# Four cross-attention layers on one core: the rest of a pair's keys in one tile, its transposes in 64 columns, and both phases in one block

## The chip, the cores and the metric

The kernel runs on one core of a Trainium2 chip. The metric is the device time of one execution in microseconds (us), the median of the runs.

## The reference

A stream x of 8 batches x 512 tokens x 512 channels goes through four cross-attention layers, each of which attends to the same context of 8 x 77 tokens of width 1024 and adds its result to the stream.

```python
# layers 0 and 2 (16 heads of 64, below "wide")
q, k, v = x @ Wq, ctx @ Wk, ctx @ Wv
logits = einsum(q, k) * 64 ** -0.5
logits[:, token_indices_A] += -20 * (1 - mask_A)      # the same for B
x = softmax(logits) @ v @ Wo + bo + x
# layers 1 and 3 (16 query heads of 32, 4 key/value heads, below "narrow")
q, k, v = rmsnorm(x) @ wq, ctx @ wk, ctx @ wv
x = softmax(q @ k.T * 32 ** -0.5) @ v @ wo + x
```

All is fp32. The kernel reaches that accuracy on TensorE by splitting each operand into a high part (fp32r, a copy by ScalarE) and a low part (the difference, by VectorE or GpSimd) and by adding three products: high x high, high x low, low x high (`three_passes`, L228).

## The kernel before

**The first block** (`context_block`, L254) computes keys and values of the context, for both wide layers in eight pairs of weight blocks and for both narrow ones in a ninth (`NJ` = 9 rounds j). A round is 96 key matmuls of 308 columns and 120 value matmuls of 256 columns. ScalarE and VectorE drain each bank into a high and a low part, and SP stores them to the scratch tensors `k_scr`, `v_scr`, `k1_scr`, `v1_scr` (L340 to L353). SP also loads the weights one round ahead (L329). In the last round it loads x of batch 0 into one half of the weight buffer (L331), then two blocks of query weights (L333, L335), of which the second waits until x has been split (`late_lo`, L334). ScalarE's queue in the last round is: drain the keys, split those two weight blocks (`split_late`, L386), drain the five value banks (L383); VectorE's has the same order, and TensorE's last group of value matmuls waits for VectorE's first drain (L519). SP waits at the end for all stores (L355, L356). The block ends on all engines.

**The second block** (`attention_block`, L545) runs the four layers. Its work is cut into units: one batch and one group of four heads, so 4 units a batch, 32 a layer, 128 in all (`NU`). Units of layers 0 and 2 are of kind A (wide, two chunks of 128 channels), those of 1 and 3 of kind B (narrow, one chunk). Each engine goes through steps s = 0 ... 129 in an order written out by hand (`STEPS`). In step s TensorE does:

- the scores of unit s, in 4 tiles of 128 tokens (`scores`), alternating over two banks. For a wide unit ScalarE writes the bias of the masked tokens into the bank first (`bias`, L939), and tile t + 2 can get its bias only when VectorE has subtracted the maximum of tile t out of the same bank (L944, L1059);
- the queries of unit s + 1 (`queries`), 24 or 12 matmuls of 512 columns, beside the first two tiles;
- the value matmuls of unit s - 2 (`values`, L790), beside the other two;
- three groups of four transposes of unit s - 1 (`turn`, L778), each group into one bank;
- the output projections of a batch (`project`, L810). For a wide batch all four, 96 matmuls, stand in one step out of four (`projections`, L145).

A unit has 4 x 77 = 308 probability columns per token, which don't fill 128-row blocks. Transposes n = 0 and 1 turn 128 columns each. What is left (26 columns of each pair of heads of a wide unit, 52 of a narrow one) goes through transpose n = 2 (`TWICE`): GpSimd copies these columns twice, side by side, into the tile `rest` (L1205, L1210), so that the transposed bank has them in its rows 0 to 63 and again in 64 to 127. ScalarE copies the whole bank as the high part (L974), VectorE replaces rows 64 to 127 by the difference (L1074). One value matmul with the high values in both halves then gives high x high and low x high, a second with the low values gives high x low. So a wide unit has 2 chunks x (3 + 2) = 10 value matmuls, a narrow one 3 + 3 + 2 = 8. The values come in from `v_scr` in small DMAs on SP (`load_vals`, L653; the list `pieces` from `value_pieces`, L64), 8 for a wide unit.

ScalarE's order in a wide step (L1014 to L1031) is: query copy 0, bias 2, query copy 1, bias 3, exponentials of tiles 0 and 1, output copy 0, transposed bank 0, bias 0 of the next step, output copy 1, bank 1, bias 1 of the next step, bank 2, exponentials of tiles 2 and 3, new x. VectorE's (L1121 to L1141) is: maximum and subtraction of tile 0, query 0, tile 1, query 1, tile 2, output 0, rest of bank 0, tile 3, rest of bank 1, output 1, rest of bank 2, sums and reciprocals, results of the projections. GpSimd multiplies the probabilities by the reciprocals (`normalise`, L1193), makes the two copies, and computes low parts of x and of weights.

Of the kernel before, what the change touches and what calls it, by code (L numbers as in the profile page):

```python
# [13 lines left out]

# [5 lines left out]
F32 = mybir.dt.float32  # L20
# [6 lines left out]
P = 128  # L27
# [30 lines left out]

TWICE = 2
# [4 lines left out]
def value_pieces(outs):  # L64

    blocks, pieces = [], []
    if outs == 2:
        for m in range(2):
            first, rest = len(blocks), len(blocks) + 1
            blocks += [(m, m), (TWICE, m)]  # L70
            row = REST_A * m + P - (PAIR - REST_A)
            pieces += [(2 * m, 0, CTX, first, 0, 2), (2 * m + 1, 0, P - CTX, first, CTX, 2),
                       (2 * m + 1, P - CTX, CTX, rest, row, 2), (2 * m + 1, P - CTX, CTX, rest, 64 + row, 1)]
        return blocks, pieces
    blocks = [(0, 0), (1, 0), (TWICE, 0)]
    for n in range(2):
        for h in range(GH):
            lo, hi = max(h * CTX, n * P), min((h + 1) * CTX, n * P + P)
            if lo < hi:
                pieces.append((h, lo - h * CTX, hi - h * CTX, n, lo - n * P, 2))  # L80
    row, t0 = 2 * P - (SC - REST_B), 2 * P - (GH - 1) * CTX
    pieces += [(GH - 1, t0, CTX, TWICE, row, 2), (GH - 1, t0, CTX, TWICE, 64 + row, 1)]
    return blocks, pieces
# [37 lines left out]
class Plan:  # L121
# [23 lines left out]
    def projections(self, s):  # L145
# [12 lines left out]
        return found  # L158

# [94 lines left out]
def context_block(nc, lasting, ctxT, kvw, k_scr, v_scr, k1_scr, v1_scr, x_in, wqA, boA, normB, masks, tokens,  # L254
# [5 lines left out]
    with ExitStack() as ctx:  # L260
# [6 lines left out]
        ctx_raw = sb("ctx_raw", [P, KC, ROWS], F32)  # L267
        ctx_s = sb("ctx_s", [P, 2, KC, ROWS], F32R)
        w_raw = sb("kvw_raw", [P, 2, PART], F32)
        k_out = sb("k_out", [P, 2, 2, ROWS], F32R)  # L270
        v_out = sb("v_out", [P, len(VROWS), 2, BLK], F32R)
        banks = [ctx.enter_context(nc.psum_tensor(f"ctx_bank{i}", [P, 512], F32)) for i in range(8)]

        w_A, x_s, ident, mean_w, mhalf = lasting.w_s, lasting.x_s, lasting.ident, lasting.mean_w, lasting.mhalf
        bias_s, bo, nw = lasting.bias_s, lasting.bo, lasting.nw
        w_s = w_A[:, 2:4]
        tok_i = sb("tok_i", [P, 8], I32)
        tok_f = sb("tok_f", [P, 2, 8], F32)

        mask_b = sb("mask_b", [P, 2, TILES], F32)  # L280
        iota_t = ctx_raw[:, 2, 0:CTX]
        cmp_t = [ctx_raw[:, 2, CTX * (1 + n):CTX * (2 + n)] for n in range(3)]

        ctx_loaded = [sem(f"ctx_loaded{n}") for n in range(KC // 2)]
        first_loaded = [sem(f"first_loaded{n}") for n in range(KC // 2)]
        first_hi, first_lo = sem("first_hi"), sem("first_lo")
        w_loaded = [sem("kw_loaded"), sem("vw_loaded")]
        ctx_hi, ctx_lo = sem("ctx_hi"), sem("ctx_lo")
        w_hi, w_lo = [sem("kw_hi"), sem("vw_hi")], [sem("kw_lo"), sem("vw_lo")]
        k_mm, v_mm = sem("k_mm"), sem("v_mm")  # L290
        k_hi, k_lo, v_hi, v_lo = sem("k_hi"), sem("k_lo"), sem("v_hi"), sem("v_lo")
        k_stored, v_stored = sem("k_stored"), sem("v_stored")
        consts, cleared, setup_loaded, chain = map(sem, ("consts", "setup_cleared", "setup_loaded", "dve_chain"))
        late_loaded = [sem("x_first"), sem("wq_first"), sem("wq_second")]
        late_hi, late_lo = sem("late_hi"), sem("late_lo")
        NV = len(VROWS)
        FULL = sum(r == P for r in VROWS)

        def late_parts(n):
            if n == 0:  # L300
                return [x_s[:, 0, h].rearrange("p k n -> p (k n)") for h in range(2)]
            return [w_A[:, n - 1, h] for h in range(2)]

        def keys_stored(j):
            return 64 * j

        def vals_stored(j):
            return 32 * j

        block = ctx.enter_context(nc.Block())  # L310

        @block.sync
        def _(sp):
            for k in range(0, KC, 2):
                sp.dma_start(w_raw[:, 0, BLK * k:BLK * (k + 2)], kvw[0][:, BLK * k:BLK * (k + 2)]).then_inc(first_loaded[k // 2], 16)
                sp.dma_start(ctx_raw[:, k:k + 2], ctxT[:, k:k + 2]).then_inc(ctx_loaded[k // 2], 16)
            sp.dma_start(w_raw[:, 1], kvw[1]).then_inc(w_loaded[1], 16)
            sp.dma_start(mask_b[:, :, :], masks).then_inc(setup_loaded, 16)
            sp.dma_start(tok_i[:, :], tokens[:, ::token_words].partition_broadcast(P)).then_inc(setup_loaded, 16)
            sp.dma_start(bo[:, :, :], boA).then_inc(setup_loaded, 16)  # L320
            sp.dma_start(nw[:, :, :], normB).then_inc(setup_loaded, 16)
            for j in range(NJ):
                for slot in range(2):
                    if j == 0 and slot == 0:
                        sp.wait_ge(first_lo, KC // 2)
                    else:
                        sp.wait_ge(w_lo[slot], j + slot)
                    if j + 1 < NJ:
                        sp.dma_start(w_raw[:, slot], kvw[2 * j + 2 + slot]).then_inc(w_loaded[slot], 16)  # L329
                    elif slot == 0:  # L330
                        sp.dma_start(w_raw[:, 0], x_in[0].rearrange("p k n -> p (k n)")).then_inc(late_loaded[0], 16)  # L331
                    else:
                        sp.dma_start(w_raw[:, 1], wqA[0, 0]).then_inc(late_loaded[1], 16)  # L333
                        sp.wait_ge(late_lo, 1)  # L334
                        sp.dma_start(w_raw[:, 0], wqA[0, 1]).then_inc(late_loaded[2], 16)  # L335
                for m in range(2):
                    sp.wait_ge(k_lo, 4 * j + 2 * m + 2)
                    for h in range(2):
                        into = k_scr[j, :, :, m, h] if j < B else k1_scr[m, :, :, h]
                        sp.dma_start(into.rearrange("b q n -> q b n"),  # L340
                                     k_out[:, m, h].bitcast(F32).rearrange("q (b n) -> q b n", b=B))\
                          .then_inc(k_stored, 16)
                sp.wait_ge(v_lo, NV * j + NV)
                if j < B:
                    sp.dma_start(v_scr[j, 0:FULL * P].rearrange("(r p) s n -> p r s n", p=P),
# [981 lines left out]
```

## Time and profile before

| | us |
|---|---|
| Runs (3) | 2134.89, 2130.80, 2132.19 |
| Median | 2132.19 |
| The profiled execution's time | 2131.65 |
| Its span in the profile | 2129.7 |
| TensorE busy | 2080.0, 98% |
| VectorE busy | 1361.5, 64% |
| ScalarE busy | 927.0, 44% |
| GpSimd busy | 690.4, 32% |
| Mean granted TensorE clock | 0.995 |

The span runs from the first to the last instruction. PE is TensorE's matmuls, PEld its weight loads, DVE VectorE, ACT ScalarE, POOL GpSimd, SPq the queue of the engine that issues DMAs. Matmuls are pipelined and their ends are modelled, so start times tell more than durations. An arrow names what an instruction waited for.

### The profile page before, as it was taken

To read this page: it belongs to the slowest core of one execution; us is meant where nothing else is said; L and a number is where in the kernel's file an instruction comes from. 1 tells how busy PE (TensorE), PEld (TensorE's weight loads), DVE (VectorE), ACT (ScalarE), POOL (GpSimd) and SP (SyncE) were. 2 spreads that over 40 slices of the span, in tenths; PEclk is the share of its full clock that TensorE was granted. 3 is DMA by queue.
4 is the path that set the end of the run, shared out by engine and by line. 5 is a ranking of instruction groups with operands and counts; after the bars stand their busy time and mean duration, and the time that the engine had idled before them with its cause. 6 is when DMAs were issued, how large, how long until landed. Compare 5 with 4: busy or idle time off the path is not lost.

```text
span 2129.7 us, 31554 instructions
## 1 busy us (share of the span) xinstructions
PE 2080.0 (98%) x11674; PEld 1795.4 (84%) x11674; DVE 1361.5 (64%) x2344; ACT 927.0 (44%) x1750; POOL 690.4 (32%) x646
## 2 busy tenths in 40 slices
PE   8999999999999998999999999999999989999998
PEld 8999978888888887788888888888888877888886
DVE  5333355765576556688888675557655765888885
ACT  3222243543354334555555453335433543555552
POOL 0000043312231245465454431223122434554441
PEclk9999999999999999999999999999999999999999
DMA  7777842222222222343333332212221222233322
GB/s 213 173 158 157 179 120 74 67 62 74 54 65 63 77 60 72 85 110 100 86 95 92 102 90 67 73 55 65 63 76 51 70 72 80 67 94 88 87 71 81
DMA packets 260729, 191.02 MB, mean 90 GB/s; under 512 B 195842, under 2 KB 198306, under 8 KB 258018
## 3 DMA queue, kind: packets, MB, share of 16 engines
q1 hardware_dynamic: 260578, 189.02, 34.0%
q8 instruction: 93, 1.52, 0.3%
q14 instruction: 58, 0.48, 0.1%
HBM read 132.66 MB, written 56.26 MB: 89 GB/s over the span
## 4 chain that ended last, share of the span: by engine, by line
PE 38%; issue 31%; POOL 12%; DVE 4%; ACT 1%; SPq 1%; DMA 0%; POOLq 0%; ACTq 0%; DVEq 0%
POOL prob L1197 6%; PE acc_bank L804 6%; PE acc_bank L230 4%; PE acc_bank L232 4%; PE acc_bank L231 4%; PE t_bank L787 4%; PE q_bank L769 3%; PE q_bank L773 3%; PE q_bank L771 3%; POOL x_s L1172 3%; POOL rest L1205 2%; PE s_bank L230 2%; PE s_bank L232 2%; PE s_bank L231 1%; DVE pT_s L1077 1%
## 5 line engine op out<-in xcount | busy, mean ns | idle before, releaser
L1197 POOL TENSOR_TENSOR prob<-prob,rinv 128x1232 f32<-128x1232 f32 x128 | 288.3, 2252 | 1034.9 <-DVE rinv L1092 1034.9
L804 PE MATMUL acc_bank<-pT_s,vals_s 128*128 128x512 f32 x1152 | 369.7, 417 | 0.0
L1055 DVE TENSOR_REDUCE mx<-s_bank 128x4 f32<-128x308 f32 x512 | 243.4, 475 | 187.9 <-PE s_bank L735 117.5
L969 ACT ACTIVATE q_s<-q_bank 128x512 fp32r<-128x512 f32 x192 | 114.8, 598 | 528.7 <-PE q_bank L773 523.6
L769 PE MATMUL q_bank<-x_s,w_s 128*128 128x512 f32 x768 | 320.5, 417 | 4.0 <-POOL w_s L1190 4.0
L773 PE MATMUL q_bank<-x_s,w_s 128*128 128x512 f32 x768 | 314.6, 410 | 0.0
L771 PE MATMUL q_bank<-x_s,w_s 128*128 128x512 f32 x768 | 314.1, 409 | 0.0
L230 PE MATMUL acc_bank<-o_s,w_s 128*128 128x512 f32 x752 | 304.4, 405 | 3.0 <-DVE o_s L1083 3.0
L232 PE MATMUL acc_bank<-o_s,w_s 128*128 128x512 f32 x752 | 298.0, 396 | 0.0
L231 PE MATMUL acc_bank<-o_s,w_s 128*128 128x512 f32 x752 | 297.6, 396 | 0.0
L960 ACT ACTIVATE prob<-prob,rstd 128x308 f32<-128x308 f32 x256 | 140.0, 552 | 288.4 <-DVE prob L1059 260.6
L1059 DVE TENSOR_TENSOR prob<-s_bank,mx 128x308 f32<-128x308 f32 x512 | 244.9, 478 | 26.8 <-DVE mx L1055 0.5
L804 PEld LDWEIGHTS acc_bank<-pT_s,vals_s 128*128 128x128 f32 x1152 | 214.5, 189 | 39.5
L1077 DVE TENSOR_TENSOR pT_s<-t_bank,pT_s 128x512 fp32r<-128x512 f32 x256 | 175.6, 686 | 89.1 <-ACT pT_s L974 89.1
L974 ACT ACTIVATE pT_s<-t_bank 128x512 fp32r<-128x512 f32 x384 | 222.1, 594 | 23.8 <-PE t_bank L787 23.8
L1106 DVE SCALAR_TENSOR_TENSOR x_back<-acc_bank,bo,x_back 128x512 f32<-128x512 f32 x64 | 48.0, 750 | 248.7 <-PE acc_bank L232 248.6
L1089 DVE TENSOR_REDUCE sums<-prob 128x16 f32<-128x1232 f32 x128 | 183.2, 1431 | 3.6 <-ACT prob L952 1.6
L230 PEld LDWEIGHTS acc_bank<-o_s,w_s 128*128 128x128 f32 x752 | 141.6, 188 | 35.7 <-DVE o_s L1083 4.8
L232 PEld LDWEIGHTS acc_bank<-o_s,w_s 128*128 128x128 f32 x752 | 141.6, 188 | 34.3
L231 PEld LDWEIGHTS acc_bank<-o_s,w_s 128*128 128x128 f32 x752 | 142.0, 189 | 31.2
L773 PEld LDWEIGHTS q_bank<-x_s,w_s 128*128 128x128 f32 x768 | 146.1, 190 | 22.8
L769 PEld LDWEIGHTS q_bank<-x_s,w_s 128*128 128x128 f32 x768 | 146.6, 191 | 19.6 <-POOL w_s L1190 4.3
(105 smaller groups left out, 4086.0 us busy)
## 6 DMA issues: line engine op xcount, KB each, us to landing
stream<-x_back SPq DMA_DIRECT2D x128, 256.0 KB, 2.6
x_front<-stream SPq DMA_DIRECT2D x96, 256.0 KB, 3.3
x_back<-stream SPq DMA_DIRECT2D x96, 256.0 KB, 3.9
kvw_raw<-kvw SPq DMA_DIRECT2D x17, 1024.0 KB, 8.6
k_scr<-k_out SPq DMA_DIRECT2D x36, 308.0 KB, 8.4
keys_s<-k_scr SPq DMA_DIRECT2D x128, 77.0 KB, 2.5
v_scr<-v_out SPq DMA_DIRECT2D x8, 1024.0 KB
x_back<-x_in SPq DMA_DIRECT2D x32, 256.0 KB, 4.1
```

The costliest lines, as they stand in the source:

```text
L230: pe.matmul(out, weights[0], moving[0], start=start, stop=False)
L231: pe.matmul(out, weights[0], moving[1], start=False, stop=False)
L232: return pe.matmul(out, weights[1], moving[0], start=False, stop=stop)
L769: pe.matmul(out, w[0], x_now[0], start=k == 0, stop=False)
L771: pe.matmul(out, w[0], x_now[1], start=False, stop=False)
L773: mm = pe.matmul(out, w[1], x_now[0], start=False, stop=k == XC - 1)
L804: mm = pe.matmul(out, w, pT_s[:, part], start=i == mine[0] and part == 2 * n and w is v[0], stop=i == mine[-1] and w is terms[-1][0] and p ...
L974: act.activation(pT_s[:, 2 * n], t_bank[(3 * u + n) % 2][:, :], ACT.Copy).then_inc(t_hi, 1)
L1055: dve.tensor_reduce(top, scored, AX_X, ALU.max).then_inc(s_max, 1)
L1059: dve.tensor_tensor(prob[:, slot, t].rearrange("q (h n) -> q h n", h=GH), scored, top.unsqueeze(2).broadcast_to([P, GH, CTX]), ALU.subtrac ...
L1077: dve.tensor_tensor(pT_s[:, 2 * n + 1], t_bank[(3 * u + n) % 2][:, :], pT_s[:, 2 * n].bitcast(F32), ALU.subtract).then_inc(t_lo, 1)
L1197: pool.tensor_tensor(view, view, rinv[:, slot].unsqueeze(2).broadcast_to([P, TILES * GH, CTX]), ALU.mult).then_inc(p_norm, 1)
```

## The change

1. **Values of a wide unit.** The tile `rest` is now 64 columns wide: 32 of each pair of heads, once. The transposed bank has them in rows 0 to 31 (pair 0) and 32 to 63 (pair 1). Each pair gets a tile of its own in `pT_s` (which grows from 5 to 6 tiles): the high part in rows 0 to 31, again in 32 to 63, the low part in 64 to 95, zeros in the last 32. The values beside it are high, low, high. One value matmul per chunk does all three products: 2 x (3 + 1) = 8. ScalarE makes four copies of 32 rows where it made one, VectorE two subtractions of 32 rows where it made one, and SP issues 10 value loads where it issued 8.
2. **Transpose n = 2 in 64 columns**, for wide units from `rest`, for narrow ones straight from `prob`. GpSimd makes one copy for a wide unit, none for a narrow one. ScalarE copies 64 rows of a narrow unit.
3. **ScalarE's order** in a wide step: the exponentials of tiles 2 and 3 stand ahead of bank 2.
4. **One block.** The context's code is cut into one function per engine, called at the head of each engine's program. The attention's tiles lie over the context's, in an order that pairs a tile with one that is dead early. SP issues the first loads of attention (`begin`) in the last but one round, ahead of that round's stores. TensorE goes on to attention when all key banks are drained and the three late splits done; other engines wait for the stores only before they write over `k_out` and `v_out`.

```diff
-            row = REST_A * m + P - (PAIR - REST_A)
-            pieces += [(2 * m, 0, CTX, first, 0, 2), (2 * m + 1, 0, P - CTX, first, CTX, 2),
-                       (2 * m + 1, P - CTX, CTX, rest, row, 2), (2 * m + 1, P - CTX, CTX, rest, 64 + row, 1)]
+            row = P - (PAIR - REST_A)
+            pieces += [(2 * m, 0, CTX, first, 0, (0, 2)), (2 * m + 1, 0, P - CTX, first, CTX, (0, 2))]
+            pieces += [(2 * m + 1, P - CTX, CTX, rest, REST_A * slot + row, parts)
+                       for slot, parts in enumerate(((0, 1), (1, 2), (0, 1)))]
...
+    def sync(sp, begin):
...
+            if j == NJ - 2:
+                begin()
             for m in range(2):
                 sp.wait_ge(k_lo, 4 * j + 2 * m + 2)
...
-        pT_s = sb("pT_s", [P, 5, TOK], F32R)
-        rest = sb("rest", [P, TILES, P], F32)
+        rest = sb("rest", [P, TILES, 2 * REST_A], F32)
+        pT_s = sb("pT_s", [P, 6, TOK], F32R)
...
+            def begin():
+                sp.wait_ge(context.k_stored, context.wide_keys)
+                sp.wait_ge(context.v_stored, context.wide_vals)
+                sp.wait_ge(keys_zeroed, 2)
+                load_keys(0)
+                load_keys(1)
+                sp.wait_ge(vals_zeroed, 2)
+                load_vals(0)
+                load_vals(1)
+                load_weights(0)
+                load_weights(1)
+                for k in range(RING):
+                    load_front(1, k)
+                for m in range(XC):
+                    load_back(0, m)
+
+            context.sync(sp, begin)
             for s in range(STEPS):
+                if s == 0:
+                    sp.wait_ge(context.k_stored, context.all_keys)
+                    sp.wait_ge(context.v_stored, context.all_vals)
...
 # TensorE, turn
-                    mm = pe.transpose(t_bank[(3 * u + n) % 2][:, t * P:t * P + P], p, ident[:, :])
+                    if n < TWICE:
+                        rows, p = P, prob[:, u % 2, t, base:base + P]
+                    else:
+                        rows, p = 64, rest[:, t] if a else prob[:, u % 2, t, SC - REST_B:SC]
+                    mm = pe.transpose(t_bank[(3 * u + n) % 2][0:rows, t * P:t * P + P], p, ident[:, :])
 # TensorE, values
+                        if n == TWICE:
+                            terms = [(v[0], 2 * n + m)] if kind(u).name == "A" else [(v[0], 2 * n), (v[1], 2 * n)]
 # TensorE, start of attention
+            context.tensor(pe)
+            pe.wait_ge(context.k_lo, context.all_drained)
+            pe.wait_ge(context.late_lo, 3)
 # TensorE, a wide step
-                    beside(scores(s, 2), v, 5)
+                    beside(scores(s, 2), v, 4)
                     turned(0)
-                    beside(scores(s, 3), v, 5)
+                    beside(scores(s, 3), v, 4)
 # ScalarE, split_t
+                if n == TWICE and kind(u).name == "A":
+                    for m in range(2):
+                        for copy in range(2):
+                            e = act.activation(pT_s[REST_A * copy:REST_A * (copy + 1), 2 * n + m],
+                                               t_bank[(3 * u + n) % 2][REST_A * m:REST_A * (m + 1), :], ACT.Copy)
+                    e.then_inc(t_hi, 1)
+                    return
 # ScalarE, a wide step
                     bias(s + 1, 1)
+                    exps(s, 1)
                     turned(2)
-                    exps(s, 1)
 # VectorE, rest_t
+                if n == TWICE and kind(u).name == "A":
+                    for m in range(2):
+                        here = slice(REST_A * m, REST_A * (m + 1))
+                        e = dve.tensor_tensor(pT_s[64:64 + REST_A, 2 * n + m], t_bank[(3 * u + n) % 2][here, :],
+                                              pT_s[here, 2 * n + m].bitcast(F32), ALU.subtract)
+                    e.then_inc(t_lo, 1)
 # GpSimd, normalise
-                    for copy in range(2):
-                        ins = pool.tensor_copy(twice[:, :, copy], ends)
+                    pool.tensor_copy(rest[:, :, :].rearrange("q t (w n) -> q t w n", w=2), ends)\
+                        .then_inc(p_gathered, 1)
```

## Rows read from the trace of the kernel before

**Rows 1.** The page, part 1: busy time, share of the span, instructions.
```profile
PE 2080.0 (98%) x11674; PEld 1795.4 (84%) x11674; DVE 1361.5 (64%) x2344; ACT 927.0 (44%) x1750; POOL 690.4 (32%) x646
```

**Rows 2.** Timeline, TensorE, a wide step: start us, duration us, engine, line, operation, operands, count.
```profile
411.72 0.23 PE L729 MATMUL s_bank<-keys_s,q_s 128*128 128x154 f32 x1
411.79 0.28 PE L732 MATMUL s_bank<-keys_s,q_s 128*128 128x154 f32 x1
411.90 0.43 PE L804 MATMUL acc_bank<-pT_s,vals_s 128*128 128x512 f32 x1
...
412.24 0.44 PE L804 MATMUL acc_bank<-pT_s,vals_s 128*128 128x512 f32 x1
...
415.82 0.60 PE L787 MATMUL t_bank<-ident,prob 128*128 128x128 f32 x4
416.25 0.60 PE L787 MATMUL t_bank<-ident,rest 128*128 128x128 f32 x4
```

**Rows 3.** Timeline, ScalarE, the same step: third bank, exponentials, bias of tile 2.
```profile
405.48 0.60 ACT L974 ACTIVATE pT_s<-t_bank 128x512 fp32r<-128x512 f32 x1
405.95 0.73 ACT L952 ACTIVATE prob<-prob 128x616 f32<-128x616 f32 x1
...
410.17 0.43 ACT L945 ACTIVATE s_bank<-bias_s 128x308 f32<-128x308 f32 x1 [1.10 <-DVE prob L1059]
```

**Rows 4.** Timeline, VectorE, the same step.
```profile
405.27 0.69 DVE L1077 TENSOR_TENSOR pT_s<-t_bank,pT_s 128x512 fp32r<-128x512 f32 x1 [0.40 <-ACT pT_s L974]
405.88 0.68 DVE L1083 TENSOR_TENSOR o_s<-acc_bank,o_s 128x512 fp32r<-128x512 f32 x1
406.59 0.69 DVE L1074 TENSOR_TENSOR pT_s<-t_bank,pT_s 64x512 fp32r<-64x512 f32 x1
...
409.66 0.48 DVE L1059 TENSOR_TENSOR prob<-s_bank,mx 128x308 f32<-128x308 f32 x1
```

**Rows 5.** Timeline, a narrow step: statistics matmuls, and two bank copies in a row.
```profile
962.27 0.95 PE L850 MATMUL q_bank<-mean_w,x_power 128*128 128x1 f32 x8
...
973.94 1.08 ACT L974 ACTIVATE pT_s<-t_bank 128x512 fp32r<-128x512 f32 x2
```

**Rows 6.** Groups by line and shape, ScalarE: count, busy us, mean ns, idle before.
```profile
L383 ACT ACTIVATE v_out<-ctx_bank 128x256 fp32r<-128x256 f32 x36 | 13.6, 384 | 65.8 <-PE ctx_bank L232 65.8
...
L383 ACT ACTIVATE v_out<-ctx_bank 104x256 fp32r<-104x256 f32 x9 | 3.5, 387 | 22.9 <-PE ctx_bank L232 22.9
```

**Rows 7.** Timeline, all engines, last two context rounds and the start of attention.
```profile
208.30 3.08 SPq L329 DMA_DIRECT2D kvw_raw<-kvw  x2
...
236.49 0.43 SPq L331 DMA_DIRECT2D kvw_raw<-x_in  x1
...
244.38 1.92 ACT L389 ACTIVATE x_s<-kvw_raw 128x2048 fp32r<-128x2048 f32 x1 [7.88 <-DMA kvw_raw<-x_in]
...
269.62 0.85 PE L864 MATMUL s_bank<-x_s 128*128 128x308 f32 x2 [7.49 <-PEq L260]
...
275.92 12.50 SPq L663 DMA_DIRECT2D vals_s<-v_scr  x16
...
277.31 0.24 PE L729 MATMUL s_bank<-keys_s,q_s 128*128 128x154 f32 x1
```

**Rows 8.** Windows: length, busy us of PE, PEld, DVE, ACT, POOL; clock, DMA share, GB/s.
```profile
220.00:228.00 8.00, 8.00 (x70) 8.00 (x69) 3.53 (x4) 3.00 (x4) 0.00 (x0) 1.00 1.00 98
228.00:236.00 8.00, 8.00 (x68) 8.00 (x67) 1.27 (x3) 2.47 (x4) 0.00 (x0) 1.00 0.02 3
```

**Rows 9.** Waits of TensorE: us in total, times, longest.
```profile
PE ctx_bank L230 <- DVE v_out L429: 0.6, 1, 0.6
```

**Rows 10.** Timeline and windows, TensorE, the way into the second narrow layer.
```profile
1726.14 0.49 PE L769 MATMUL q_bank<-x_s,w_s 128*128 128x512 f32 x1 [1.98 <-POOL w_s L1190]
...
1728.00:1730.00 2.00, 2.00 (x8) 1.71 (x7) 1.20 (x3) 0.00 (x0) 1.68 (x1) 0.50 0.81 258
...
1732.99 0.34 PE L729 MATMUL s_bank<-keys_s,q_s 128*128 128x154 f32 x1 [1.01 <-ACT s_bank L945]
```

More of the change, by code:

```diff
@@ L15 @@
+from collections import namedtuple
 from contextlib import ExitStack
@@ L259, in context_block, with sb, sem @@
     assert NJ == B + 1
+    early = ExitStack()
+    def sb(name, shape, dt):
+        return early.enter_context(nc.sbuf_tensor(name, shape, dt))
+    def sem(name):
+        return ctx.enter_context(nc.semaphore(name))
+    ctx_raw = sb("ctx_raw", [P, KC, ROWS], F32)
+    ctx_s = sb("ctx_s", [P, 2, KC, ROWS], F32R)
+    w_raw = sb("kvw_raw", [P, 2, PART], F32)
+    k_out = sb("k_out", [P, 2, 2, ROWS], F32R)
+    v_out = sb("v_out", [P, len(VROWS), 2, BLK], F32R)
+    banks = [early.enter_context(nc.psum_tensor(f"ctx_bank{i}", [P, 512], F32)) for i in range(8)]
@@ new lines, in context_part @@
+    w_A, x_s, ident, mean_w, mhalf = lasting.w_s, lasting.x_s, lasting.ident, lasting.mean_w, lasting.mhalf
+    bias_s, bo, nw = lasting.bias_s, lasting.bo, lasting.nw
+    w_s = w_A[:, 2:4]
+    tok_i = sb("tok_i", [P, 8], I32)
+    tok_f = sb("tok_f", [P, 2, 8], F32)
+    mask_b = sb("mask_b", [P, 2, TILES], F32)
+    iota_t = ctx_raw[:, 2, 0:CTX]
+    cmp_t = [ctx_raw[:, 2, CTX * (1 + n):CTX * (2 + n)] for n in range(3)]
+    ctx_loaded = [sem(f"ctx_loaded{n}") for n in range(KC // 2)]
+    first_loaded = [sem(f"first_loaded{n}") for n in range(KC // 2)]
@@ new lines, in tensor, with keys, values @@
+    def tensor(pe):
+        def keys(n, k):
+            m, h = n // 2, n % 2
+            mm = three_passes(pe, banks[n][:, 0:HALF],
+                              [w_s[:, 0, s, BLK * k + m * P:BLK * k + m * P + P] for s in range(2)],
+                              [ctx_s[:, s, k, h * HALF:(h + 1) * HALF] for s in range(2)],
+                              k == 0, k == KC - 1)
+            if k == KC - 1:
+                mm.then_inc(k_mm, 1)
+        def values(r, j):
+            if NV * j + r >= 4:
+                pe.wait_ge(v_lo, NV * j + (1 if r == 4 else 0))
+            for k in range(KC):
+                mm = three_passes(pe, banks[4 + r % 4][0:VROWS[r], 0:BLK],
+                                  [ctx_s[:, s, k, r * P:r * P + VROWS[r]] for s in range(2)],
+                                  [w_s[:, 1, s, BLK * k:BLK * (k + 1)] for s in range(2)],
+                                  k == 0, k == KC - 1)
+            mm.then_inc(v_mm, 1)
+        for k in range(KC):
+            if k % 2 == 0:
+                pe.wait_ge(first_lo, k // 2 + 1)
+            pe.wait_ge(ctx_lo, k + 1)
+            for n in range(4):
+                keys(n, k)
+        for j in range(NJ):
+            if j:
+                pe.wait_ge(w_lo[0], j)
+                pe.wait_ge(k_lo, 4 * j)
+                for n in range(4):
+                    for k in range(KC):
+                        keys(n, k)
+            pe.wait_ge(w_lo[1], j + 1)
+            for r in range(NV):
+                values(r, j)
@@ L275, in context_block @@
[L275 to L308, printed above, removed]
@@ L1215, in root @@
                 pool.tensor_tensor(rstd[:, gb % 2], ms[:, gb % 2], mhalf[:, :], ALU.pow).then_inc(rstd_ready, 1)
+            context.gpsimd(pool)
+            pool.wait_ge(context.chain, context.chain_end)
             for slot in range(2):
```

532 lines of the change are left out of this document (250 added, 282 removed).

## The prediction, made before the changed kernel was run

> **What bounds the kernel now.** The page's first part comes first: TensorE is busy 98% of the span, VectorE 64% [rows 1]. Modelled matmul ends make that share unsafe, so the second view is the order in time inside one step of a wide (16-head) layer. There TensorE runs without a pause: from one value matmul to the next, with one score matmul between, 0.34 us (411.90 to 412.24); a score matmul alone 0.11 (411.79 to 411.90); so a value matmul is worth 0.23. Four transposes take 0.43 us (415.82 to 416.25), 0.108 each [rows 2]. In these steps work taken off TensorE is time, provided that the other queues keep up. How far they are behind is the third view, ScalarE's and VectorE's instructions of the same step [rows 3, 4]. TensorE needs the third score tile's bias to be in its bank; ScalarE wrote it from 410.17 to 410.60, and TensorE's matmul that needs it starts at 411.72 [rows 2, 3]. So there are only 1.12 us of slack, and the bias waits for VectorE (its tile-0 subtraction ends at 410.14) [rows 4].
>
> **Part 1, TensorE in wide layers.** A wide unit has 8 value matmuls instead of 10. There are 64 wide units: 128 x 0.23 = 29.4 us less TensorE work.
>
> **Part 2, transposes with 64 columns.** The third group of four transposes of each of the 128 units turns 64 columns, not 128. Which side of a transpose costs the 0.108? The statistics matmuls move one column against 128 loaded weight columns, and eight of them still span 0.95 us, about 0.11 each [rows 5]. So at this width the weight load sets the pace. What 64 loaded columns cost no row shows. Bounds: 0.108 (nothing gained, if the moving side of a transpose is as slow) and half of that, 0.054. I take 0.06, since one-column matmuls show no moving cost: 4 x 0.048 = 0.19, say 0.18 us a unit, 11.5 us over 64 wide and 11.5 over 64 narrow units. Of the narrow ones some ten, at the start of each narrow layer and at the end, wait for VectorE anyway: 54 x 0.18 = 9.7 us.
> The Trainium skill (TensorE: Matmul & The Clock Gate, "LDWEIGHTS") says that a weight load takes its columns divided by 1.2 GHz, whatever the rows; for 128 columns that is 107 ns, and the trace agrees with 108 [rows 2]. By it 64 columns would take an estimated 53 ns, and this part would come to 14 and 12 us instead of 11.5 and 9.7.
>
> **Part 3, the split of the rest in wide units.** This runs against the change. Before, ScalarE makes one copy of the third transposed bank and VectorE one subtraction. Now ScalarE makes four copies, each of 32 partitions x 512, and VectorE two subtractions of 32 x 512; the last half of the exponentials goes ahead of the copies, and VectorE's sums still stand behind its subtractions. Do fewer partitions cost less? No: ScalarE's 104x256 copy took 387 ns and its 128x256 copy 384 [rows 6]; VectorE's subtraction over 64 partitions (406.59) and over 128 (405.27) both took 0.69 [rows 4]. Back to back two ScalarE copies take 1.08, so each further one adds 0.49 [rows 5].
> Walk the chain in the step of rows 3 and 4. At 405.48 ScalarE now starts the exponentials, 0.73 long less the 0.12 by which its instructions overlap (0.60 long, 0.49 apart), so 0.61, then four copies: 405.48 + 0.61 + 3 x 0.49 + 0.60 = 408.16. VectorE, which took up the rest at 406.59, takes it up at 408.18: 1.59 late. The second subtraction adds 0.61 (405.27 to 405.88): 2.20 late. Sums, reciprocals and the next tile 0 follow in its queue, so the bias of tile 2 is done at 410.60 + 2.20 = 412.80. TensorE reached the step's end earlier: the chain starts 0.46 earlier (two value matmuls; 412.34), TensorE's wish for scores 2 comes 0.64 earlier (also the transposes; 411.08). A stall of 412.34 - 411.08 = 1.26 us per step, where there was none. What is queued behind the waiting score matmul on TensorE: the value matmuls, the transposes of the unit before, and through them ScalarE and VectorE; nobody catches up by it, because VectorE's other tiles follow TensorE.
> The stall appears where VectorE comes late into a step. In wide layers the projections of a batch stand in one step of every four (96 matmuls x 0.23 = 22 us), behind which VectorE is idle again; the step after it has no stall. Three in four steps stall, and the first ones of a wide layer not: 2 x 23 x 1.26 = 58.0 us. Together with parts 1 and 2: wide layers 58.0 - 29.4 - 11.5 = +17.1 us. Units 30 and 31 of each wide layer carry the long split into narrow steps: +1.
> Bounds for the four copies: if each took only the 0.36 of the 308-column work (a bias of 0.43 less the usual overlap), the stall is 0.74 and the wide layers -7; if copies of one bank don't overlap (0.60 each), 1.7 and +37.
> GpSimd: one copy less in wide units, two less in narrow ones, 0.37 each. Its normalisation starts 2.2 later, ends before TensorE's transposes need it (they are later by the stall as well). Cost nothing. Two more value loads per wide unit on SP, 0.78 us each (16 in 12.50 [rows 7]): ten take 7.8, the keys 1.2, in a step of over 11, and values are loaded a whole step ahead; nothing.
>
> **Part 4, one block.** Now TensorE idles 7.49 us between the blocks, from 262.13 to 269.62, and the first score of attention is at 277.31 [rows 7]. Without the gap, and with the two openers (0.3) and 24 query matmuls at 0.23 (5.5): 267.8, 9.5 us less; the slow restart is in that. But the loads that attention needs are now issued by SP at the last but one key/value pair, behind the weight load that it issues up to 211.4: 20 value DMAs (15.6 us at 0.78), 4 for keys and 9 of 256 KB (some 2.5 and 4.2), so until about 233.7 [rows 7]. SP stores the keys of that pair only then. Before, these stores were through by 228, at 98 GB/s; then the DMA engines were idle until 236 [rows 8]. Now four stores of 308 KB start at 233.7 behind the last 256 KB loads: 1.23 MB at 98 to 150 GB/s is 8 to 12 us, so the value store and the load of x_in, issued at 236.49 and landed at 244.38 before [rows 7], come 8 to 11 us late. Behind x_in hang its split, then the last weight load, its split, and only then VectorE's drain of the last values, and TensorE already waits for that drain now (0.6 us) [rows 9]. So TensorE idles some 9 us before its last 24 context matmuls, and restarts at the lower clock as it does now (+2): -9.5 + 9 + 2 = +1.5. Bounds: -9.5 (the stores hide in the idle stretch) and +6 (13 us late).
> The Trainium skill (DMA: Bandwidth & Descriptors, "Queues, rings and completion order") says that a ring is consumed in order and a completion counts only after every earlier write. If x_in passed the stores, part 4 would be -9.5; by the rule it can't.
>
> **The sum.** 17.1 + 1 - 9.7 + 1.5 = +9.9 us on the profiled execution's 2131.65 (its span is 2129.7), so 2141.6. That execution is 0.54 under the median of 2132.19: 2142.
>
> **Rivals.**
> A. The stall never comes and TensorE stays the bound: -29.4 - 11.5 - 9.7 + 1.5 = -49.1, 2083 us; faster. For it: today's waits in wide steps are nearly nil. Against: the slack is 1.12 us and the added queue work 2.20. It decides at a delay under 0.9 us. Chance 0.22.
> B. The forecast. Own range 2133 to 2158. Chance 0.42.
> C. The stores hide, part 4 brings its 9.5: 2131, no change. Against: SP's queue order. Chance 0.12.
> D. The transposes cost what they did: the stall is 1.08, 46 x 1.08 - 29.4 + 1 + 1.5 = +22.8, 2155. Chance 0.14.
> E. The stalls cost TensorE's clock. A gap of 1.98 us was followed by 1728 to 1730 at 0.50, the 1.2 GHz level; a gap of 1.01 was not [rows 10]. The low stretch is longer than those 2 us; put at 3.2, half pace costs 1.6 us; in a third of 46 stalls +25, in all +74: 2167, up to 2215. Chance 0.10.
>
> **How the numbers follow.** Predicted: B, 2142. The range leaves out the upper part of E (0.06) and the fastest half or more of A (0.14): 2090 to 2175. Under 0.2% (4.3 us) this kernel's measurement tells nothing from no change. Slower: most of B (0.34), D, E: 0.58. Same: half of C, a little of B: 0.10. Faster: A, half of C, the low end of B: 0.32.
>
> **What would show it.** Value matmuls 1024 instead of 1152. In a wide step without projections: TensorE waits 1.3 us for ScalarE's bias ahead of the third score tile, VectorE waits about 1.6 us for the fourth ScalarE copy ahead of its rest subtraction, a step is 1.26 - 0.64 = 0.6 us longer than before; the step after projections 0.6 shorter. The third transposes take 0.25 us instead of 0.43, and a narrow step is 0.18 shorter. At the join TensorE has its gap ahead of the last value group of the context, not behind it, and x_in lands near 253. Wrong would be: no wait at the third tile (A), the wait there but under 0.8 us, or x_in landing before 246 (C).

## The result, and the profile after

The kernel before took 2132.04 us (2130.80 to 2134.89, 4 runs), the changed kernel **2189.14 us** (2188.57 to 2193.20, 4 runs): ratio 1.0272, 95% interval 1.0260 to 1.0284. It is slower, by 57 us; forecast were 2142 us and a range of 2090 to 2175. The profiled execution took 2188.87 us, its span is 2186.8.

Part 1 of the page, beside [rows 1]. There are 128 TensorE instructions fewer (11674 to 11546), TensorE's busy time falls by 16 us, and its share of the span from 98 to 94%: it now waits.
```profile
PE 2064.0 (94%) x11546; PEld 1770.2 (81%) x11546; DVE 1393.8 (64%) x2408; ACT 1037.1 (47%) x1942; POOL 622.0 (28%) x455
```
The waits (who waits at which line <- who releases it: us in total, times, longest) name the places: 46 waits at the first matmul of a score tile (L758), where the kernel before has 4, 3.3 us in all. 25 of them are in the first wide layer and 21 in the second; those four are among them, so 42 stalls are new, where 46 were forecast. The other lines are VectorE's 63 waits for ScalarE's copies of the rest (L1125), and at the join 12.8 us ahead of the last value group, where [rows 9] show 0.6.
```profile
DVE pT_s L1125 <- ACT pT_s L1018: 120.3, 63, 2.5
PE s_bank L758 <- ACT s_bank L984: 63.1, 46, 2.2
PE ctx_bank L237 <- DVE v_out L440: 13.4, 2, 12.8
```
The first matmuls of the first and of the third score tile in one wide step, of the kernel before (the step of [rows 2]). From the first tile at 404.75 to what follows the step's last transposes, at 416.61, are 11.86 us.
```profile
404.75 0.32 PE L729 MATMUL s_bank<-keys_s,q_s 128*128 128x154 f32 x1
...
411.72 0.23 PE L729 MATMUL s_bank<-keys_s,q_s 128*128 128x154 f32 x1
```
And after: first tile at 405.65, that of the next step at 418.68, so the step is 13.03 us. From the first tile to the third, at 414.14, are 8.49 us, where the same work took 6.97 before: 1.52 longer, of which the records show 1.35 as a wait. The rest transposes ahead of the step take 0.36 us, from 405.29 to 405.65, and before also 0.36 (416.25 in [rows 2] to 416.61).
```profile
405.29 0.60 PE L820 MATMUL t_bank<-ident,rest 128*64 128x128 f32 x4
405.65 0.32 PE L758 MATMUL s_bank<-keys_s,q_s 128*128 128x154 f32 x1
...
414.14 0.34 PE L758 MATMUL s_bank<-keys_s,q_s 128*128 128x154 f32 x1 [1.35 <-ACT s_bank L984]
...
415.85 0.60 PE L820 MATMUL t_bank<-ident,prob 128*128 128x128 f32 x4
...
418.68 0.32 PE L758 MATMUL s_bank<-keys_s,q_s 128*128 128x154 f32 x1
```
ScalarE in that step, beside [rows 3]: exponentials, four copies in 2.38 us, and a bias that waits 3.68 us for VectorE.
```profile
406.38 0.72 ACT L991 ACTIVATE prob<-prob 128x616 f32<-128x616 f32 x1
406.99 2.38 ACT L1018 ACTIVATE pT_s<-t_bank 32x512 fp32r<-32x512 f32 x4
409.38 0.60 ACT L1008 ACTIVATE q_s<-q_bank 128x512 fp32r<-128x512 f32 x1
413.66 0.43 ACT L984 ACTIVATE s_bank<-bias_s 128x308 f32<-128x308 f32 x1 [3.68 <-DVE prob L1109]
```
VectorE, beside [rows 4]: it is idle for 1.93 us, until the fourth copy ends; the two subtractions, the sums, the reciprocals and the next tile 0 come behind. That is the whole chain.
```profile
409.39 1.38 DVE L1125 TENSOR_TENSOR pT_s<-t_bank,pT_s 32x512 fp32r<-32x512 f32 x2 [1.93 <-ACT pT_s L1018]
410.81 1.44 DVE L1144 TENSOR_REDUCE sums<-prob 128x16 f32<-128x1232 f32 x1
412.28 0.25 DVE L1147 RECIPROCAL rinv<-sums 128x16 f32<-128x16 f32 x1
412.56 0.48 DVE L1105 TENSOR_REDUCE mx<-s_bank 128x4 f32<-128x308 f32 x1
413.15 0.48 DVE L1109 TENSOR_TENSOR prob<-s_bank,mx 128x308 f32<-128x308 f32 x1
```
How much each stage lost: one score matmul's weight loads, with first and last start, in the first and in the second wide layer. The three numbers behind the count are the shortest, the median and the longest in ns. Before:
```profile
L735 PEld LDWEIGHTS s_bank<-keys_s,q_s x256: 187/190/330, 278.2 to 812.5; 128*128 128x128 f32 x128
L735 PEld LDWEIGHTS s_bank<-keys_s,q_s x256: 187/190/333, 1184.1 to 1736.6; 128*128 128x128 f32 x128
```
After:
```profile
L764 PEld LDWEIGHTS s_bank<-keys_s,q_s x256: 187/192/333, 283.2 to 843.6; 128*128 128x128 f32 x128
L764 PEld LDWEIGHTS s_bank<-keys_s,q_s x256: 187/192/338, 1218.9 to 1790.9; 128*128 128x128 f32 x128
```
Start +5.0; wide layers 534.3 to 560.4 and 552.5 to 572.0, together **+45.6**; narrow layers with their transitions, 371.6 to 375.3 and 393.1 to 395.9, +6.5. The sum is the span's +57.1.

The join, beside [rows 7]: the 20 value loads go out from 214.25, the key stores from 232.14 and take 8.5 us to issue; x_in, issued at 236.49 before, goes out at 245.03 and is split at 256.80 (before: 244.38). TensorE's gap is now 12.84 us, and the first score matmul is at 282.24 (before: 277.31).
```profile
214.25 13.33 SPq L684 DMA_DIRECT2D vals_s<-v_scr  x20
...
232.14 8.51 SPq L355 DMA_DIRECT2D k_scr<-k_out  x4
...
245.03 1.07 SPq L344 DMA_DIRECT2D kvw_raw<-x_in  x1
...
256.80 1.92 ACT L401 ACTIVATE x_s<-kvw_raw 128x2048 fp32r<-128x2048 f32 x1 [20.83 <-DMA kvw_raw<-x_in]
...
271.55 0.54 PE L237 MATMUL ctx_bank<-w_s,ctx_s 128*104 128x256 f32 x1 [12.84 <-DVE v_out L440]
...
282.24 0.23 PE L758 MATMUL s_bank<-keys_s,q_s 128*128 128x154 f32 x1
```

### The profile page after: what moved, and what is told of

Its sections match the earlier page's. It is cut to its first block, busy times and chain, and to the rows that moved or that the text cites. A ratio compares the mean times of both kernels' runs of the same rounds, so it can differ in the third digit from the quotient of the medians.

```text
span 2186.8 us, 31356 instructions
## 1 busy us (share of the span) xinstructions
PE 2064.0 (94%) x11546; PEld 1770.2 (81%) x11546; DVE 1393.8 (64%) x2408; ACT 1037.1 (47%) x1942; POOL 622.0 (28%) x455
## 3 DMA queue, kind: packets, MB, share of 16 engines
q8 instruction: 92, 1.51, 0.3%
## 4 chain that ended last, share of the span: by engine, by line
PE 44%; issue 33%; POOL 10%; DVE 6%; ACT 3%; SPq 2%; DMA 1%; POOLq 0%; DVEq 0%; ACTq 0%
PE acc_bank L840 6%; POOL prob L1254 5%; PE acc_bank L237 4%; PE acc_bank L239 4%; PE acc_bank L238 4%; PE t_bank L820 4%; PE q_bank L802 3%; PE q_bank L798 3%; PE q_bank L800 3%; POOL x_s L1229 3%; PE ctx_bank L237 3%; PE ctx_bank L238 3%; PE ctx_bank L239 3%; PE s_bank L237 2%; PE s_bank L239 1%
## 5 line engine op out<-in xcount | busy, mean ns | idle before, releaser
L840 PE MATMUL acc_bank<-pT_s,vals_s 128*128 128x512 f32 x1024 | 341.0, 418 | 0.0
L840 PEld LDWEIGHTS acc_bank<-pT_s,vals_s 128*128 128x128 f32 x1024 | 192.2, 191 | 28.7
L1023 ACT ACTIVATE pT_s<-t_bank 128x512 fp32r<-128x512 f32 (+1 forms) x320 | 183.0, 589 | 24.0 <-PE t_bank L820 23.9
L758 PE MATMUL s_bank<-keys_s,q_s 128*128 128x154 f32 x512 | 134.4, 262 | 63.1 <-ACT s_bank L984 63.1
L984 ACT ACTIVATE s_bank<-bias_s 128x308 f32<-128x308 f32 x256 | 111.5, 436 | 162.0 <-DVE prob L1109 162.0
L820 PE MATMUL t_bank<-ident,prob 128*128 128x128 f32 (+1 forms) x1280 | 185.8, 274 | 1.2 <-DVE pT_s L1132 1.2
L820 PEld LDWEIGHTS t_bank<-ident,prob 128*128 128x128 f32 (+1 forms) x1280 | 155.6, 137 | 28.6 <-DVE pT_s L1132 1.6
L758 PEld LDWEIGHTS s_bank<-keys_s,q_s 128*128 128x128 f32 x512 | 97.7, 191 | 92.2 <-ACT s_bank L984 82.5
```

The costliest lines, as they stand in the source:

```text
L758: pe.matmul(cols, q_s[:, slot, 0, c, tok], keys[:, c, 0], start=False, stop=False, skip_group_check=True)
L820: mm = pe.transpose(t_bank[(3 * u + n) % 2][0:rows, t * P:t * P + P], p, ident[:, :])
L840: mm = pe.matmul(out, w, pT_s[:, part], start=i == mine[0] and part == 2 * n and w is v[0], stop=i == mine[-1] and w is terms[-1][0] and p ...
```

## The experiments

The theory: the wide layers' loss is one chain, ScalarE's four copies, VectorE's subtractions, its sums, the next tile 0, the bias. Rival 1: ScalarE's queue as a whole is too long. Rival 2: TensorE is slower in these steps by itself. Ratios are to the kernel before, which ran again beside each group of experiments, with medians of 2130.93 to 2132.50 us, so a difference between two groups is good to some 1.5 us.

**Sums first.** In VectorE's wide steps of the kernel after:
```
-                    turned(2)
                     denominators(s)
+                    turned(2)
```


> One change on the kernel after: in a wide step VectorE does the sums and reciprocals of this unit ahead of the two 32-row subtractions of the unit before. The theory (the stall is VectorE's: it waits for the fourth ScalarE copy, and sums, reciprocals and the next tile 0 stand behind that wait): the sums now run while the copies are made, so the next tile 0 comes about 1.8 us earlier, the chain is 2.65 - 1.8 = 0.9 us late, within the 1.12 of slack, and the 46 stalls of 1.5 us go. A step is then 11.86 - 0.46 = 11.4 us; total 2132 - 29.4 (128 value matmuls) + 4.9 (join) + some starts = 2109 to 2115 us. Rival 1 (ScalarE's own queue, two or three instructions longer, is what makes the bias late): its queue is the same, so the stall stays over 1.2 us and the time at 2185 to 2190. Rival 2 (the step is longer since TensorE's matmuls run slower in it): unchanged, 2189.

Measured: **2109.88 us** (2108.02 to 2111.57), ratio 0.9894 (0.9879 to 0.9908). One line moved takes 79 us off the kernel after and makes it faster than the kernel before. VectorE now sums while the copies are made, and waits 0.30 us:
```profile
408.95 1.43 DVE L1144 TENSOR_REDUCE sums<-prob 128x16 f32<-128x1232 f32 x1
410.41 0.25 DVE L1147 RECIPROCAL rinv<-sums 128x16 f32<-128x16 f32 x1
410.96 1.38 DVE L1125 TENSOR_TENSOR pT_s<-t_bank,pT_s 32x512 fp32r<-32x512 f32 x2 [0.30 <-ACT pT_s L1018]
412.38 0.48 DVE L1105 TENSOR_REDUCE mx<-s_bank 128x4 f32<-128x308 f32 x1
```
The waits at L758 are 5, 3.9 us in all. TensorE's fourth tile is at 404.75 and that of the next step at 416.13: a step of 11.38 us, 0.48 less than before (forecast for the two value matmuls: 0.46). Against it a stalled step of the kernel after is 13.03 - 11.38 = 1.65 us longer; the listed wait is only 1.35 of that. Both rivals predicted no change, and both fall.
```profile
404.75 0.32 PE L758 MATMUL s_bank<-keys_s,q_s 128*128 128x154 f32 x1
...
406.87 0.60 PE L820 MATMUL t_bank<-ident,rest 128*64 128x128 f32 x4
407.22 0.32 PE L758 MATMUL s_bank<-keys_s,q_s 128*128 128x154 f32 x1
...
416.13 0.32 PE L758 MATMUL s_bank<-keys_s,q_s 128*128 128x154 f32 x1
```

**Two copies of 64 rows,** and the rest of wide units transposed in 128 columns again. GpSimd makes one copy more for it, and VectorE's subtractions read other rows of the bank; shown is ScalarE's part:
```
-                        for copy in range(2):
-                            e = act.activation(pT_s[REST_A * copy:REST_A * (copy + 1), 2 * n + m],
-                                               t_bank[(3 * u + n) % 2][REST_A * m:REST_A * (m + 1), :], ACT.Copy)
+                        e = act.activation(pT_s[0:64, 2 * n + m], t_bank[(3 * u + n) % 2][64 * m:64 * m + 64, :],
+                                           ACT.Copy)
```


> The kernel after with ScalarE's four copies of 32 rows made two of 64: the rest stands twice in 128 columns, both copies of one head pair next to each other (GpSimd makes one copy more), the third group of wide units is transposed with 128 columns, VectorE's two subtractions stay. Queue orders as in the kernel after. Theory: two copies fewer take 1.2 us off the delay of 2.65, the stall falls from 1.5 to 0.3 us, 46 x 1.2 = 55 us: 2134 us. If the transposes with 64 columns had been cheaper (the prediction: 0.18 us a unit), this would cost 64 x 0.18 = 11.5 us: 2145; if they cost the same, as the trace of the kernel after reads, nothing, and the third four transposes take the same 0.36 us start to next in both kernels. A 64-row copy: 0.60 us; if it overlaps its follower by 0.1 as one of 128 rows does, the two take 1.08, if not 1.19. Rival 1 (number of ScalarE instructions): also faster, told apart by e1. Rival 2 (TensorE slower in itself): 2189 or more.

Measured: 2134.92 us (2133.02 to 2136.54), ratio 1.0012 (1.0003 to 1.0022). The 46 waits are still there, 12.7 us in all, so 0.28 us each instead of 1.37. A step is 11.85 us (third tile at 404.77 and at 416.62), 1.18 shorter than in the kernel after, and two copies take 1.19 where four took 2.38: the chain is shorter by just the two copies. Four rest transposes with 128 columns take 0.36 us to the next matmul (408.95 to 409.31), with 64 columns 0.35 (406.87 to 407.22, above): no gain from fewer columns. The pair of 64-row copies takes 1.19 us; the instruction behind it starts at 411.74, 0.09 before its end.
```profile
408.95 0.60 PE L820 MATMUL t_bank<-ident,rest 128*128 128x128 f32 x4
409.31 0.32 PE L758 MATMUL s_bank<-keys_s,q_s 128*128 128x154 f32 x1
```
```profile
410.64 1.19 ACT L1017 ACTIVATE pT_s<-t_bank 64x512 fp32r<-64x512 f32 x2
411.74 1.14 ACT L965 ACTIVATE x_s<-x_front 128x512 fp32r<-128x512 f32 x2
```

**Exponentials after the copies:**
```
-                    exps(s, 1)
                     turned(2)
+                    exps(s, 1)
```


> The kernel after with ScalarE's order of the kernel before: the second half of the exponentials behind the four copies. Theory: VectorE takes up the rest when the fourth copy ends, 0.6 to 0.7 us sooner; sums then still find their exponentials done (they run beside the subtractions). Delay 2.65 - 0.7 = 1.95, stall 0.8 instead of 1.5, 46 x 0.7 = 32 us: 2157 us. Rival 1 (ScalarE's queue as a whole): the same instructions in another order, 2189. If the exponentials end up behind VectorE's second subtraction, the gain is smaller, down to 2175.

Measured: 2158.24 us (2156.47 to 2160.39), ratio 1.0120 (1.0103 to 1.0137); 46 waits, 36.6 us, 0.80 each. The same instructions on ScalarE in another order take 31 us off: the length of its queue as a whole (rival 1) isn't the limit, the place of the copies is. So the one reordering inside the change (its part 3) cost 31 of the 57 us.

**The join alone:** one block, with the kernel before's handling of the rest.

> Part 4 of the change alone: one block, loads for the attention issued in the last but one round of the context part; the rest is handled as in the kernel before (10 value matmuls, rest doubled in 128 columns, one copy and one subtraction, exponentials after the copy). Theory: the join costs what the first score's place shows, 282.24 against 277.31, so 2132 + 5 = 2137 us, and no stalls at the third score tile (before: 4 of them, 3.3 us in all). Rival: one block costs or gives something elsewhere too (the places of the buffers, semaphores): outside 2134 to 2140. The three other parts would then be worth 2189 - 2137 = 52 us together.

Measured: 2134.51 us (2132.76 to 2136.61), ratio 1.0010 (1.0000 to 1.0019). The first score matmul is at 282.42, 5.1 us later than before; the span is only 2.1 longer, because the wide layers are 1.9 and the narrow ones 1.2 shorter. Why is open. The three other parts of the change together cost 2189.1 - 2134.5 = 54.6 us.

**The attention's loads later:** SP calls begin() in the last round, behind the key stores, not in the last but one.

> The kernel after, with the 36 loads for the attention issued by SP in the last round of the context part, behind its key stores, instead of in the last but one. Theory (the join's cost is SP's issue order: these loads hold up the stores and, behind them, the load of x_in): x_in lands at 244.4 again (after: 256.8), the gap of 12.8 us before the last value group goes, the two openers follow the last context matmul at about 262.2 and the first score matmul is at 267.8 to 270 (after: 282.24): 12 to 14 us less, 2175 to 2177. Rival (one block brings nothing, because the loads then come too late: 36 issues take some 20 us from 256, so the first keys land by 259 but query weights and later x wait): first score on time, but a new wait in the first two units, 2180 or more. The 46 stalls stay at 1.4 us, 63 us in all.

Measured: 2182.14 us (2181.34 to 2183.89), ratio 1.0241 (1.0226 to 1.0257), 7.0 less than after, where 12 to 14 were expected. The place is right: x_in is issued at 236.57, the 12.8 us gap is gone (the longest wait of that kind is 2.0), and the first score matmul is at 268.23. But half of the 14 us is given back. The rival said so of the first units; the wait is another than it named, at the transposes of unit 0:
```profile
PE t_bank L820 <- POOL prob L1254: 9.8, 1, 9.8
```
GpSimd zeroes rows of the transposed rest only once the value stores have landed (a wait in its code ahead of that line), its first normalisation is queued behind that, and the stores now go out behind all the loads:
```profile
262.95 12.81 SPq L684 DMA_DIRECT2D vals_s<-v_scr  x20
...
280.44 1.51 SPq L366 DMA_DIRECT2D v_scr<-v_out  x2
```

**All edits:** sums first, two copies, late loads.

> One block with the late loads, 8 value matmuls, VectorE's sums ahead of its rest subtractions, and two ScalarE copies of 64 rows instead of four of 32. Theory: the sums-first kernel's 2109.9 less the join's 12 to 14 is 2096 to 2098; two copies fewer (1.2 us less ahead of each projection and narrow start) may give 1 to 3 more: 2094 to 2098 us, no stall at a third score tile, a wide step of 11.38 us. Rival (the join's gap only hid other starts, or the two gains overlap): 2102 or more.

Measured: 2099.38 us (2098.96 to 2100.64), ratio 0.9853 (0.9838 to 0.9868), 1 us over the expected end, with the same wait at the first transposes (9.1 us).

**The loads in two parts:** keys behind the key stores, the others behind the last value stores, weights and x ahead of the values; all edits otherwise.

> The kernel of all edits (2099.4), with SP's loads for the attention in two parts: the keys of units 0 and 1 behind the key stores of the last round, everything else behind the last value stores. Its trace showed the join's gap gone (first score matmul at 267.6), but a new wait of 9.1 us ahead of the first transposes: GpSimd zeroes rows of the transposed rest only when the value stores have landed, these were issued from 278 behind the 33 loads, and its normalisation of unit 0 stands behind that. Theory: the stores go out from 263 again and land by about 270, GpSimd is free in time, the 9.1 us go, nothing new is late (values of unit 0 are wanted some 20 us after they land): 2089 to 2091. Rival (the loads themselves are now late: 20 value loads of 0.6 us and 9 others end at some 287): a wait of 3 us or more ahead of the first value matmuls or of the next batch's queries, 2094 or more.

Measured: **2093.80 us** (2091.77 to 2093.99), ratio 0.9824 (0.9807 to 0.9840), the fastest kernel of this case, 38 us under the kernel before. The 9.1 us are gone; 1.5 us came in their place (a wait for the keys of unit 2, now behind all the other loads), and around that wait TensorE's granted clock averages 0.83 and 0.74 over 8 us, so part of them ran at the 1.2 GHz level (8 - 4 x 0.83 - 4 x 0.74 = 1.7 us). Against the kernel of all edits TensorE is 7.3 us ahead at the rest transposes of unit 1 (310.10 there, 302.78 here) and still so near the end of the first wide layer (786.29, 778.95). Behind the next wait, 1.98 us for weights in both kernels, the granted clock is 0.77 and 0.80 over 8 us here and 1.00 there: 1.7 us, and the 5.6 us between the two times are what is left.
```profile
290.11 0.31 PE L761 MATMUL s_bank<-keys_s,q_s 128*128 128x154 f32 x1 [1.50 <-DMA keys_s<-k_scr]
```
```profile
288.00:292.00 4.00, 2.50 (x11) 0.83 0.99 283
292.00:296.00 4.00, 4.00 (x18) 0.74 0.52 142
```

**The join alone, with this order of loads:**

> Part 4 alone (one block, the rest handled as in the kernel before) with the same order of SP's loads. Theory: part 4 gives what it can when the stores are not held up: the first score matmul at 267.8 instead of 277.31, 2131.5 - 9.5 - 2 (the few waits that the join alone also lost) = 2120 to 2123. Rival (one block with its loads inside can't gain, something of the start is only moved into the first units): 2128 or more.

Measured: 2123.72 us (2122.34 to 2124.79), ratio 0.9964 (0.9951 to 0.9977). The first score matmul is at 267.93. One block was worth 7.8 us; with its loads in the last but one round the same block cost 2.0 (the join alone, above). The rival, 2128 or more, falls.
```profile
267.93 0.23 PE L760 MATMUL s_bank<-keys_s,q_s 128*128 128x154 f32 x1
```

**Control: sums first in the kernel before.**

> A control: the kernel before with VectorE's sums ahead of its one rest subtraction in wide steps. Theory (there VectorE doesn't wait for ScalarE at this point, and TensorE is the bound): no change, 2130 to 2134; at most the 3.3 us of its four waits at the third score tile go. Rival (sums first makes any of these kernels faster, and the 79 us that it gave the kernel after are not the chain's): clearly faster, by 20 us or more.

Measured: 2129.59 us (2127.14 to 2132.32), ratio 0.9992 (0.9983 to 1.0002): no change that can be told. The order of the sums is worth nothing where VectorE doesn't wait for the copies.

**Copies of all 128 rows.**

> A price: the kernel with two copies, where each of the two copies takes all 128 rows of the bank instead of 64 of them (what it writes is not the reference's rest; all else is the same). Two copies of 64 rows took 1.19 us, without the overlap of 0.1 us that ScalarE's 128-row copies show. If fewer rows are what loses the overlap, these two take 1.08 us; if it is that both read one bank, 1.19 again. Total within 5 us of 2135 either way.

Measured: the pair takes 1.08 us from the same bank, so reading one bank is not what loses the overlap. The single time, 2126.20 us, is 9 below 2135, more than expected: with a chain 0.11 us shorter 9 waits are left of 46, 5.8 us of 12.7. It is one execution, and the size isn't settled by it.
```profile
409.59 1.08 ACT L1017 ACTIVATE pT_s<-t_bank 128x512 fp32r<-128x512 f32 x2
```
Few rows alone don't lose it either. In the narrow steps of the kernel after, a 64-row copy stands behind a 128-row one of another bank: the two take 1.06 us, and the next instruction starts 0.11 before their end. What the 32-row copies and the pair of 64-row copies have that this one hasn't (a neighbour that is as small, from the same bank, on other rows) was not tried in parts, so the cause is open.
```profile
L1023 ACT ACTIVATE pT_s<-t_bank x2: 585/588/592, 903.2 to 903.7; 128x512 fp32r<-128x512 f32 x1, 64x512 fp32r<-64x512 f32 x1
```
```profile
903.18 1.06 ACT L1023 ACTIVATE pT_s<-t_bank 128x512 fp32r<-128x512 f32 x2
904.13 0.62 ACT L976 ACTIVATE xsq<-x_front 128x512 f32<-128x512 f32 x1
```

## Why the prediction was wrong

The sign and the mechanism of the stall were right; four terms were mis-sized, all the same way: together 47 us between +9.9 and +57.1.

- **Part 1**, -29.4 us, holds: with the stalls gone a step is 0.48 us shorter (forecast 0.46), and the two wide layers are 31.6 us shorter than before.
- **Part 2 failed.** The step "I take 0.06" a transpose was wrong: 64 loaded columns cost what 128 did, 0.35 to 0.36 us for four, and a narrow step is 10.53 us in both kernels (below, before and after; the x8 are both groups in one). The weight loads did become shorter in the records (111 ns on average, against 141 for 128 columns in the two-copies kernel), but a transpose moves 128 columns as well, and the one-column statistics matmuls [rows 5] showed only that a weight load can set the pace, not that the moving side is free. Whether the moving side or something fixed sets it now, no run tells. It was rival D, given 0.14. Cost of the error: 9.7 us in narrow layers; in wide ones 11.5, of which the stall gives back 46 x 0.18 = 8.3, so 3.2. The rule of the Trainium skill for a weight load (TensorE: Matmul & The Clock Gate, "LDWEIGHTS"), by which an estimated 14 and 12 us were to be had, doesn't give the time of these transposes.
```profile
973.25 0.60 PE L787 MATMUL t_bank<-ident,prob 128*128 128x128 f32 x4
...
983.78 0.60 PE L787 MATMUL t_bank<-ident,prob 128*128 128x128 f32 x4
```
```profile
964.26 1.03 PE L820 MATMUL t_bank<-ident,prob 128*128 128x128 f32 x8
...
974.79 1.03 PE L820 MATMUL t_bank<-ident,prob 128*128 128x128 f32 x8
```
- **Part 3: right chain, stall too short.** Forecast 1.26 us, measured 1.65 (13.03 - 11.38): 46 x 0.39 = 18 us. The step that failed is "each further one adds 0.49": that is the pitch of 128-row copies. The 32-row ones took 0.60 each, 2.38 for four, where the sum had 2.07; and VectorE's two 32-row subtractions took 1.42 up to the sums, where it had 1.30. That is 0.43; the transposes that did not get shorter take 0.18 back, which makes 1.51, and the third tile does come 1.52 late. The rest lies behind it: from the third tile to the fourth are 2.07 us (414.14 to 416.21), in the sums-first kernel 1.95 (414.18 to 416.13), a term that the prediction doesn't have. So wide layers: 17.1 + 18 + 11.5 = 46.6, measured 45.6, and that fit is partly luck. Only 42 stalls are new, which is 7 us less, and four steps lose 2.8 to 3.4 us against the sums-first kernel instead of 1.65, nearly 6 more: two of them are followed by a lower clock (rival E below), the last with projections of each wide layer has a wait of 1.41 us for VectorE's part of the outputs, 0.30 before. "If copies of one bank don't overlap (0.60 each)" stood as a bound with a stall of 1.7 and +37. Its size was right for the copies, its reason wasn't: 128-row copies of one bank do overlap. Its sum was off: the forecast has the last of the four at 0.60 already, so three times 0.11 make a stall of 1.59, and +32.
- **Units 30 and 31, and the narrow layers**: +1 and -9.7 forecast, +6.5 measured. Without the transposes' gain 5.5 us are left over. Waits at the narrow scores for VectorE grew from 12.3 to 19.5 us. Most of that is one wait at the start of each narrow layer, 4.38 and 4.50 us, where the kernel before has 2.14 twice. With the sums first they are 2.74 twice, with two copies at most 3.3: it is the same late VectorE, carried into the narrow steps. The step that failed is the +1 for units 30 and 31.
- **Part 4**: +1.5 forecast, +5.0 measured at the first score, inside its bound of +6. The step "come 8 to 11 us late" was 12.4, since SP needed 8.5 us to issue four stores and 4.2 for the two value stores. Landing order, the gap's new place and its cause are as forecast; its -9.5 is what the last join kernel got (277.31 to 267.93).
- **Rival A** (the stall never comes) is the sums-first kernel: 2109.9, not 2083, since the transposes' 21.2 us were not to be had and the join cost 3.5 more (2083 + 24.7 = 2107.7). **Rival E** fell in its size: of the regular stalls two were followed by a clock partly at the 1.2 GHz level, not 15 or all. After the wait of 1.85 us at 313.09 it is 0.70 and 0.88 in 312 to 320 (below, columns as in [rows 8] for TensorE alone), and 0.57 in 1300 to 1304, after 1.72 us; the steady waits of 1.35 us have 1.00 behind them. That is some 3.4 us. Over the span 4 us windows below 1.00 lose 21 us, in the kernel before 11; 3 of these 10 lie between 260 and 276, at the join, and others around the starts of the narrow layers.
```profile
308.00:312.00 4.00, 3.25 (x17) 1.00 0.21 61
312.00:316.00 4.00, 2.91 (x11) 0.70 0.02 6
316.00:320.00 4.00, 4.00 (x28) 0.88 0.25 79
```
- **The range.** The bounds that were written down, all unfavourable at once: copies at 0.60 +37 for the wide layers, no gain from the transposes 3.2 more there and 0 instead of -9.7 in the narrow ones, units 30 and 31 +1, join +6: +47, 2179 us, and 2175 with the bound's sum put right. So the range nearly held all that had a bound. The measured time lies above even that, since three terms had none: VectorE's subtractions and the time behind the wait (46 x 0.13 = 6 us over the stall of 1.52 that this sum has), and the starts of the narrow layers, 4.5 us over their +1.

## What to carry to other kernels

When work moves off the bound engine and onto the queues of others, write down what stands behind the new wait and what of it doesn't need it: here the sums needed nothing from the copies, and moving one line was worth 79 us, more than the whole change had lost. Don't price several small copies in a row by the pitch of full-size ones: here they took their full length each. And give a bound to every term, also to one that is put at +1 or at nothing: the terms without one are what carried the time beyond the range.

## What the runs showed of the hardware

- ScalarE: two 128x512 copies in a row take 1.08 us, two of 64 rows 1.19, four of 32 rows 2.38; each group from one bank. A copy's own length, 0.58 to 0.60, doesn't depend on its rows. A single 64-row copy between two full-size instructions overlaps both by 0.11 (two in 1.06). VectorE's 32x512 subtractions: 0.69 each, two in 1.38; the 128x512 ones start 0.60 to 0.61 after each other.
- TensorE: four transposes of 128x128 and of 128x64 both hold it for 0.35 to 0.36 us up to the next matmul.
- A listed wait of 1.35 us was a loss of 1.65 us per step: the stretch around a wait has to be compared, not the wait alone.
- The time that SP needs to issue a transfer isn't fixed: the 1 MB value store took it 0.36 us in the kernel before and 2.78 behind the late key stores, so a delay of the issues adds to that of the transfers.
- The same wait of 1.98 us for weights, at the same place, is followed by a granted clock of 1.00 in the kernel of all edits and of 0.77 and 0.80 over 8 us in the one with the loads in two parts.
